# Attention and gated FFN in one kernel on eight cores: one softmax bound per half of the heads, its root on GpSimd, and the output's tanh with a buffer of its own

## The reference

```
xn = layernorm(x)
latent = xn @ Wc_down                       # 1024 -> 512
q = (latent @ Wq_up)                        # 512 -> 16 heads of 64
k, v = split(latent @ Wkv_up)               # one head of 64 each
s = (softmax(causal(q k^T / 8)) v) @ Wc_proj
h = silu(xn @ wg^T) * (xn @ wu^T)           # 1024 -> 3072, integer weights / 127
g = silu(h @ wd^T)                          # 3072 -> 1024
out = x + s * g
```

## Time and profile before

| what | value |
|---|---|
| median of 3 runs | 1435.1 us |
| the profiled execution's own time | 1433.0 us |
| its span on the slowest core (core 5) | 1431.5 us |
| spans of the eight cores | 1425.5 to 1431.5 us |
| mean granted TensorE clock of the cores | 0.991 to 0.996 |
| TensorE, ScalarE, VectorE, GpSimd busy | 94%, 84%, 48%, 14% |

### The profile page before, as it was taken

The page is one execution under the profiler, slowest core; times in us unless marked ns, Lnnn a source line. Parts: engine busy times, 40 slices in busy tenths (PEclk is TensorE's granted clock), DMA queues, the critical chain, the costliest instruction groups (busy, mean ns, idle before and its releaser), DMA issues.

```text
span 1431.5 us, 44899 instructions; the slowest of 8 cores (1425.5 to 1431.5 us)
## 1 busy us (share of the span) xinstructions
PE 1351.5 (94%) x18064; PEld 821.1 (57%) x18064; DVE 689.8 (48%) x1325; ACT 1200.9 (84%) x1254; POOL 203.2 (14%) x355
## 2 busy tenths in 40 slices
PE   2699999999999999999999999999999999999997
PEld 2466565565655656556556556555555655555553
DVE  3677786677764655535334325333423243333234
ACT  3666678777879797997997996999899999999993
POOL 2322121212212221101001211000002020000010
PEclk9999999999999999999999999999999999999999
DMA  9835474476948661321321532222135132212031
GB/s 235 154 99 147 114 177 128 120 182 164 239 121 234 159 219 54 134 70 45 132 94 57 160 105 86 80 72 73 47 110 163 46 115 79 78 66 75 2 112 52
DMA packets 64762, 164.68 MB, mean 115 GB/s; under 512 B 7728, under 2 KB 15152, under 8 KB 64560
## 3 DMA queue, kind: packets, MB, share of 16 engines
q1 hardware_dynamic: 52272, 131.26, 27.8%
q0 software_dynamic: 12288, 30.54, 11.7%
HBM read 151.42 MB, written 33.55 MB: 129 GB/s over the span
## 4 chain that ended last, share of the span: by engine, by line
PE 84%; ACT 4%; DVE 4%; issue 3%; DMA 2%; POOL 1%; DVEq 0%; ACTq 0%; POOLq 0%; SPq 0%
PE ps L236 82%; ACT p_sb L963 3%; PE ps L247 2%; DMA wc_sb<-wc 2%; POOL p_dg L971 1%; ACT p_dg L963 1%; DMA xt<-xb 1%; DVE bnd L576 0%; DVE st L387 0%; DVE st L390 0%; DVE acc_sb L868 0%; DVE p_dg L971 0%; ACT xnT L476 0%; ACT t_sb L866 0%; DVE acc_sb L876 0%
## 5 line engine op out<-in xcount | busy, mean ns | idle before, releaser
L963 ACT ACTIVATE p_sb<-ps,nbias 128x1024 bf16<-128x1024 f32 x1024 | 1068.2, 1119 | 129.9 <-PE ps L236 128.3
L236 PEld LDWEIGHTS ps<-vaug,p_sb 128*128 128x128 bf16 x8192 | 314.3, 97 | 151.7 <-issue 75.6
L236 PE MATMUL ps<-own_f,wgu_sb 128*128 128x512 bf16 x1536 | 386.5, 380 | 1.6 <-issue 0.4
L236 PE MATMUL ps<-vaug,p_sb 128*128 128x65 bf16 x8192 | 362.3, 193 | 13.8 <-ACT p_sb L963 6.4
L236 PE MATMUL ps<-qT,kT 64*128 64x256 bf16 (+1 forms) x4352 | 329.2, 269 | 5.9 <-ACT p_sb L963 3.5
L236 PEld LDWEIGHTS ps<-qT,kT 64*128 64x128 bf16 x4352 | 164.9, 94 | 136.5 <-issue 105.6
L236 PEld LDWEIGHTS ps<-own_f,wgu_sb 128*128 128x128 bf16 x1536 | 128.3, 98 | 130.6 <-issue 23.5
L236 PE MATMUL ps<-wdr,h_sb 128*128 128x512 bf16 x768 | 196.4, 380 | 0.0
L714 DVE COPY g_sb<-ps 128x512 f32<-128x512 f32 x96 | 66.2, 689 | 169.0 <-PE ps L236 168.8
L236 PEld LDWEIGHTS ps<-wdr,h_sb 128*128 128x128 bf16 x768 | 61.7, 97 | 65.2 <-issue 17.1
L716 ACT ACTIVATE t_sb<-g_sb 128x512 f32<-128x512 f32 x96 | 60.6, 632 | 36.8 <-DVE g_sb L714 31.8
(11 more groups left out here) (102 smaller groups left out, 1023.0 us busy)
## 6 DMA issues: line engine op xcount, KB each, us to landing
wgu_sb<-wgub SPq DMA_DIRECT2D x72, 512.0 KB, 3.3
xt<-xb SPq DMA_DIRECT2D x57, 512.0 KB, 6.1
wdr<-wdb SPq DMA_DIRECT2D x72, 256.0 KB, 4.0
wgu_sb<-wgu POOLq DMA_DIRECT2D x24, 512.0 KB, 7.0
wgub<-wgu_sb SPq DMA_DIRECT2D x24, 512.0 KB, 6.2
out<-acc_sb POOLq DMA_DIRECT2D x27, 256.0 KB, 4.1
wdr<-wd POOLq DMA_DIRECT2D x24, 256.0 KB, 8.5
wdb<-wdr SPq DMA_DIRECT2D x24, 256.0 KB, 5.8
```

The lines of the kernel that those rows point to most:

```text
L236: return p.op("tensor", lambda e: e.matmul(out, lhsT, rhs, start=start, stop=stop, skip_group_check=shared), waits, "pe" if tok else None, ...
L963: ex = A(cost, lambda en, dst=dst, src=src, bias=bias: en.activation(dst, src, AF.Exp, bias=bias, scale=0.125), [mm, p_prior(u)[1], bias_t ...
```

## The change

It has three parts and some constants that follow from them.

First, the bound. The squares of each half of the heads are multiplied once with 128 columns of `halves_sb` that hold ones for even heads in the first 64 columns and for odd heads in the last 64, so that the upper half of the partitions gets the sums of one parity and the lower half those of the other. The maxima go to a bf16 tile `bndb`; a product with the identity shifted by 64 columns (`ident_sb` grows to 192 columns) turns the halves, and the maximum of both is what the two sums gave before. A factor of 1.01 covers the rounding to bf16. Second, for slots 2 to 15 the root is computed on GpSimd with six instructions. Third, the tanh of the FFN output has a buffer `t2_sb` of its own and is written before the step that looks for the operands of the rest; its product on VectorE is put in the queue when the tanh is expected to be done, and one such tanh is open at a time. The ring of down weights goes from 10 to 9, `PE_WORK` from 1195e3 to 1191e3.

```diff
-DR = 10
+DR = 9
...
-PE_WORK = 1195e3
+PE_WORK = 1191e3
...
     wd_d = nc.dram_tensor("wd", [24, 128, 1024], I32, kind="ExternalInput")
-    ident_d = nc.dram_tensor("ident", [128, 128], BF16, kind="ExternalInput")
+    ident_d = nc.dram_tensor("ident", [128, 192], BF16, kind="ExternalInput")
     halves_d = nc.dram_tensor("halves", [128, 256], BF16, kind="ExternalInput")
...
     teffv = sbuf("teffv", [128, DK, HD], BF16)
-    ident_sb = sbuf("ident_sb", [128, 128], BF16)
+    ident_sb = sbuf("ident_sb", [128, 192], BF16)
     halves_sb = sbuf("halves_sb", [128, 256], BF16)
...
     t_sb = sbuf("t_sb", [128, 512], F32)
+    t2_sb = sbuf("t2_sb", [128, 512], F32)
     g_sb = sbuf("g_sb", [128, 2, 512], F32)
...
     bnd = sbuf("bnd", [128, 2, 12], F32)
+    bndb = sbuf("bndb", [128, 2, 2], BF16)
     nbias = sbuf("nbias", [128, 2, 2], F32)
...
         def TP(out, in_, waits=(), tok=False):
-            return p.op("tensor", lambda e: e.transpose(out, in_, ident_sb[:, :]),
+            return p.op("tensor", lambda e: e.transpose(out, in_, ident_sb[:, 0:128]),
                         waits, "pe" if tok else None, 56.0)
...
         load_x(1)
-        t_id = DMA(ident_sb[:, :], ident_d[:, :], "c_id", 32)
+        t_id = DMA(ident_sb[:, :], ident_d[:, :], "c_id", 48)
         t_wc = DMA(wc_sb[:, :, :], wc_d.ap().rearrange("(k p) l -> p k l", p=128), "w_c", 2048, engine="gpsimd")
...
             for half in range(2):
-                for o in range(2):
-                    yield lambda: max(ready(sq, t_hv), bank_t())
-                    b, fr = take()
-                    mm = MM(bank(b), halves_sb[:, o * 128:(o + 1) * 128],
-                            sq_sb[:, half * 512:(half + 1) * 512], True, True,
-                            [sq, t_hv] + fr, tok=True)
-                    red = V(690, lambda en, b=b, half=half, o=o: en.reduce_max(
-                        bnd[:, par, half * 2 + o:half * 2 + o + 1], bank(b), axis=AX.X),
-                        [mm, bnd_free[par]])
-                    give(b, [red])
+                yield lambda: max(ready(sq, t_hv), bank_t())
+                b, fr = take()
+                mm = MM(bank(b), halves_sb[:, 64:192], sq_sb[:, half * 512:(half + 1) * 512], True, True,
+                        [sq, t_hv] + fr, tok=True)
+                red = V(690, lambda en, b=b, half=half: en.reduce_max(
+                    bndb[:, par, half:half + 1], bank(b), axis=AX.X), [mm, bnd_free[par]])
+                give(b, [red])
             sq_free[0] = mm
-            yield lambda: ready(kmx_tok.get(e))
+
+            yield lambda: max(ready(red, kmx_tok.get(e)), bank_t())
+            b, fr = take()
+            turned = MM(bank(b)[:, 0:2], ident_sb[:, 64:192], bndb[:, par, :], True, True, [red, t_id] + fr, tok=True)
 
             B = bnd[:, par, :]
-            q2 = B[:, 0:4].rearrange("p (h o) -> p h o", o=2)
             pr = B[:, 4:6]
...
             t = B[:, 8:10]
-            a = V(265, lambda en: en.tensor_tensor(pr, q2[:, :, 0], q2[:, :, 1], ALU.max), [red])
-            a = V(265, lambda en: en.tensor_scalar(pr, pr, kmx[:, e + 1:e + 2], 1.0 / 128.0,
+            a = V(265, lambda en, b=b: en.tensor_tensor(pr, bank(b)[:, 0:2], bndb[:, par, :], ALU.max), [turned])
+            give(b, [a])
+            a = V(265, lambda en: en.tensor_scalar(pr, pr, kmx[:, e + 1:e + 2], 1.01 / 128.0,
                                                    ALU.mult, ALU.mult), [a, kmx_tok[e]])
-            a = V(265, lambda en: en.tensor_single_scalar(
-                y.bitcast(I32), pr.bitcast(I32), 1, ALU.arith_shift_right), [a])
-            a = V(265, lambda en: en.tensor_scalar(y.bitcast(I32), y.bitcast(I32), MAGIC, -1,
-                                                   ALU.subtract, ALU.mult), [a])
-            a = V(265, lambda en: en.tensor_tensor(t, y, y, ALU.mult), [a])
-            a = V(265, lambda en: en.scalar_tensor_tensor(t, t, -0.5, pr, ALU.mult, ALU.mult), [a])
-            a = V(265, lambda en: en.scalar_tensor_tensor(y, t, 1.5, y, ALU.add, ALU.mult), [a])
-            a = V(265, lambda en: en.scalar_tensor_tensor(nbias[:, par, :], y, -1.0, pr, ALU.mult, ALU.mult),
-                  [a, qT_free[par]])
+            if e < 2:
+                a = V(265, lambda en: en.tensor_single_scalar(
+                    y.bitcast(I32), pr.bitcast(I32), 1, ALU.arith_shift_right), [a])
+                a = V(265, lambda en: en.tensor_scalar(y.bitcast(I32), y.bitcast(I32), MAGIC, -1,
+                                                       ALU.subtract, ALU.mult), [a])
+                a = V(265, lambda en: en.tensor_tensor(t, y, y, ALU.mult), [a])
+                a = V(265, lambda en: en.scalar_tensor_tensor(t, t, -0.5, pr, ALU.mult, ALU.mult), [a])
+                a = V(265, lambda en: en.scalar_tensor_tensor(y, t, 1.5, y, ALU.add, ALU.mult), [a])
+                a = V(265, lambda en: en.scalar_tensor_tensor(nbias[:, par, :], y, -1.0, pr, ALU.mult, ALU.mult),
+                      [a, qT_free[par]])
+            else:
+                yi, nb = y.bitcast(I32), nbias[:, par, :]
+                a = P(230, lambda en: en.tensor_scalar(yi, pr.bitcast(I32), -0.5, float(MAGIC), ALU.mult, ALU.add), [a])
+                a = P(230, lambda en: en.tensor_tensor(t, y, y, ALU.mult), [a])
+                a = P(230, lambda en: en.tensor_tensor(t, t, pr, ALU.mult), [a])
+                a = P(230, lambda en: en.tensor_scalar(t, t, 0.5, -1.5, ALU.mult, ALU.add), [a])
+                a = P(230, lambda en: en.tensor_tensor(t, t, y, ALU.mult), [a])
+                a = P(230, lambda en: en.tensor_tensor(nb, t, pr, ALU.mult), [a, qT_free[par]])
             bias_tok[e] = a
...
         t_free = [None]
+        t2_free = [None]
+        t2_busy = [False]
         acc_free = [None] * 4
...
                 fetch(e, nh)
             yield lambda: 0.0
+            sm = av if bd is None else bank(bd)
+            yield lambda: INF if t2_busy[0] else 0.0
+            t2_busy[0] = True
+            t2 = A(480, lambda en: en.activation(t2_sb[:, :], sm, AF.Tanh, scale=SCALE3), [acc, t2_free[0]])
+            yield lambda: ready(t2)
 
             if e < LB and (e, nh) not in fetched:
...
                 part, res = s_last[:, e - LB, cols], xo_last[:, e - LB, cols]
                 t_part, t_res = s_spill.get((e, nh)), xo_last_tok[e - LB]
-            sm = av if bd is None else bank(bd)
-            t2 = A(480, lambda en: en.activation(t_sb[:, :], sm, AF.Tanh, scale=SCALE3), [acc, t_free[0]])
             dst = av if direct else keep[:, e - (NG - 2), nh * 512:(nh + 1) * 512]
-            t_free[0] = u1 = V(690, lambda en: en.scalar_tensor_tensor(
-                dst, t_sb[:, :], 1.0, sm, ALU.add, ALU.mult),
+            t2_free[0] = u1 = V(690, lambda en: en.scalar_tensor_tensor(
+                dst, t2_sb[:, :], 1.0, sm, ALU.add, ALU.mult),
                 [t2, None if direct else own_f_free[0], acc_free[tt] if bd is not None else None])
+            t2_busy[0] = False
             acc_free[tt] = u1
             if bd is not None:
...
         "wgu": np.ascontiguousarray(wgu), "wd": np.ascontiguousarray(wdt),
-        "ident": np.eye(128, dtype=ml_dtypes.bfloat16),
+        "ident": np.concatenate([np.eye(128), np.eye(128)[:, 0:64]], axis=1).astype(ml_dtypes.bfloat16),
         "halves": halves.astype(ml_dtypes.bfloat16),
```

## The result

The changed kernel takes 1414.98 us (median of 4 runs, 1413.17 to 1416.68), the kernel before, beside it on the same chip, 1435.05 us. The ratio is 0.9863, 95% interval 0.9849 to 0.9878: about 20 us faster.

What follows compares the result with a forecast made beforehand. The prediction took TensorE to bound the kernel. Its terms, -6.9 + 1.6 - 0.5 - 2.0 + 0.5 = -7.3 us, took the median of 1435.1 to 1427.8, forecast as 1428 us, range 1420 to 1435.

Steps and rivals of the forecast that it cites:

- The bound: Whole kernel: TensorE sets the time, busy 1351.5 of 1431.5 us, with ScalarE a near second.
- Sums per half of the heads: Row blocks' products of squares: 32 fewer on TensorE at 0.216 us each, 6.9 us saved.
- The 4.2 us of the other spacing: Products of squares: the saving estimated if 512-column products were spaced at the sustained 131 ns.
- The turn: 16 new two-column products with a shifted identity on TensorE: cost 1.6 us, between 0.5 and 6.1.
- What VectorE's relief is worth: TensorE's waits on VectorE: 70 to 86 us of relief priced at 2.8%, a gain of 2.0 us.
- The bound of 9.6 us: Upper limit for the worth of VectorE's relief: half of TensorE's 19.2 us of waits on VectorE.
- The tanh: FFN output: three quarters of VectorE's 56.5 us standing still, 42 us, taken away.
- The fear of the shared port: Root steps on GpSimd could hold up VectorE's two-input instructions: up to 16 us of VectorE's time.
- a loss by more batches: Rival, score products: the newly written order breaks batches, 0.2 us each, 10 us lost for 50, 1438 us; chance 0.12.
- The third rival: VectorE's relief worth the 9.6 us bound plus some of the 9.9 us on exps: -14, 1421 us; chance 0.13.

Runs made afterwards that it cites:

- h1: Kernel before, order kept, 32 products of squares and 32 reductions of the second parity left out: 0.9954, 6.6 us less.
- h3: Changed kernel, order kept, root of all row blocks emitted on VectorE while GpSimd is booked: 0.9914, 1.0052 of the changed kernel.
- i4: Changed kernel, TensorE's and ScalarE's order kept, product of the output's tanh queued on VectorE together with the tanh: 0.9918, 1.0056 of the changed kernel.
- i5: Changed kernel, order kept, each of the 32 reductions made twice, the second unbooked: 1.0019, 1.0158 of the changed kernel.
- i1: Kernel before, order kept, second parity's products and reductions left out and root of row blocks 2 to 15 on GpSimd: 0.9948, 7.5 us less.
- h2: Kernel before, order kept, root of row blocks 2 to 15 emitted on GpSimd while VectorE is booked: 0.9970, 4.3 us less.
- f3: Changed kernel with the tanh and its product written together into the shared buffer again, order of its own: 0.9888, 1.0025 of the changed kernel.
- h4: Changed kernel, order kept, each of the 32 products of squares and 32 reductions made twice: 1.0028, 1.0167 of the changed kernel.
- g1: Changed kernel with PE_WORK 1195e3 instead of 1191e3, same work, order of its own: 0.9901, 1.0039 of the changed kernel.

## Why the prediction was wrong

**The bound** was read rightly. TensorE's stream sets the time; no run moved ScalarE's work. But the list of its waits left out 4.1 us for mask products on GpSimd, of which 3.5 went with the new placing of the masks; no term stood for them.

**Sums per half of the heads.** The removed stream was forecast at 6.9 us and measured at 6.6 (h1, 4.2 to 8.9 by its interval). The 4.2 us of the other spacing lie at the lower end of that interval, and 0.216 us is the nearer. (That other spacing is the 131 ns of the Trainium skill, TensorE: Matmul & The Clock Gate, Back-to-back issue gap.) The turn was priced at 1.6 us; the changed kernel shows one wait of 2.6 us for the reduction, and 0.169 us in flight. Nothing here is off by more than 2 us, though TensorE's busy time fell by 4.1 us and not by some 7.

**The step that failed is "What VectorE's relief is worth", 2.0 us.** It took TensorE's waits on VectorE per busy us of VectorE, 2.8%, for the price of a us of VectorE's time. In one and the same order, putting the root back on VectorE cost 7.4 us for 22 us (h3), the product queued early 8 us for 15 us of standing still (i4), and 32 unbooked reductions 22 us for 22 us (i5): 30 to 100%, not 3%. The reason shown by i5 is place: what VectorE's small steps delay is what TensorE's list has next (the turn, the normalised output), and everything behind waits with it. An average over all of VectorE's time, most of which nobody waits for, says nothing on those instructions. The bound of 9.6 us was too low as well, since it allowed no wait that the profile did not already have.

These prices hold in the order of the changed kernel. In the order of the kernel before, the same term would have been about right: its root and reductions together, some 44 us of VectorE's time, brought 0.6 us beyond the stream (i1, 7.5 less 6.9) and the root alone 4.3 (h2). So the 2.0 us were worked out for a list that the change replaces. What the forecast lacked is the step from the old order to one that is written for the moved work.

The reverse is not symmetrical. Where the planner books VectorE's time and VectorE needs less (h1, i1), the order has nothing to put there: 22 us of reductions left out brought nothing beyond the stream. Lateness against the booked time costs; being early gained 0 to 4.3 us. 4.3 us for the root in the kernel before (h2), where VectorE is late 56.5 us over 30 tanhs, fit this, but that the tanhs are the reason was only argued.

**The tanh.** 42 of the 56.5 us of standing still were to go; 8.7 went. The mechanism is right all the same (i4): its worth was underrated and its size overrated. In an order of its own the same part shows as 3.6 us (f3), within the noise.

**The root on GpSimd.** The fear of the shared port didn't come true: the mask product's mean is 450 ns, before 469, and TensorE's waits on VectorE fell, in a kept order too (h2). There, with the same 116 mask products on VectorE, they took 56.5 us in all, before 56.9. The rule of the Trainium skill (SBUF — State Buffer, Who interferes with whom) is not refuted by this. It says what happens when two such instructions meet. Here steps of 0.2 to 0.3 us, 84 in 1413 us, may simply not have met VectorE's two-input instructions often enough to be seen; how often they met was not counted.

**The order.** The forecast gave its rewriting no share in the likeliest case, and 0.12 to a loss by more batches. Two pairs of runs have the same operations and differ by order (and by the engine of a few small ones, such as two and four mask products): root on GpSimd in the kernel before, 1.0053 against 0.9970 (12 us); root on VectorE in the changed kernel, 1.0012 against 0.9914 (14 us). So an order is worth up to 1%, as much as most of the change. Batches are not how: the changed kernel's list has 569 batches of score products, 65 of them of one unit, the kernel before's 546 with 23, and it is the faster, though the rival's price of 0.2 us makes this a loss of 4.6 us. The rival was wrong in its mechanism, and the uncertainty that it stood for was far too small. The third rival, that VectorE was worth more, came nearest. It had 0.13, and by its own terms it adds up to -14.9 us and 1420, not to -14 and 1421.

**The sum after the fact.** From the changed kernel, in its order: the root 7.4, the queueing of the product 8, the stream of the products 6.9 less 1 for the turns. That is 21 us, and 20 were measured. The near match is partly luck: each of the first two terms is known to 3 or 4 us only, the third was not measured in this order, and i1 and h4 show that such terms need not add up. From the kernel before, in its order: products and root together 7.5 us. The first sum would say that the content explains the whole, the second says that products and root explain a third; the tanh's part was not run in the old order. The likely reason for the difference, argued and not shown, is that an order is made for the work that it books. How much of the 20 us a best order for the old content could have had stays open; the runs show only that its neighbours are 0 to 14 us worse.

## What to carry to other kernels

In a kernel whose order is written by a planner, a part tried alone is measured together with a new order, worth up to 1% here; keep the order (book the old work, emit the new) to learn what the edit itself is worth, and only then let the planner write again and tune its constants. Price relief of a half idle engine by what stands directly behind its instructions in the bound engine's list, not by its average share of waits. In these runs an engine that was later than booked cost a third to all of its delay, and one that was earlier gained at most a fifth of its relief. And a row of waits can cost more than its length: in g1 the products behind it ran at half the granted clock.

## What was not expected of the hardware

The six steps of the root have means of 210 to 309 ns on GpSimd in the changed kernel; the integer one is the longest there, and the shortest is shown last:

```profile
L609 POOL TENSOR_SCALAR bnd<-bnd 128x2 f32<-128x2 f32 x14 | 3.3, 233 | 2.2 <-POOL bnd L608 2.2
...
L610 POOL TENSOR_TENSOR bnd<-bnd 128x2 f32<-128x2 f32 x14 | 2.9, 210 | 2.1
```

That is not fixed by the operation. The same six have 192 to 229 ns in the kernel before with its order kept (h2), where the integer one is

```profile
L624 POOL TENSOR_SCALAR bnd<-bnd 128x2 int32<-128x2 int32 x14 | 3.2, 229 | 71.3 <-DVE bnd L608 65.7 <-DVE den L1044 5.7
```

and 309 in the changed kernel. What makes the difference stays open.

The same step for the layer norm's root took 0.19 us. On VectorE these steps take 0.16 to 0.17 us, two of them in the earlier trace rows. So GpSimd needs 1.2 to 1.9 times as long for them, and the move still gained in a kept order.
